# A macaron block of three stages in one kernel: flags summed behind the gate projection, products of the high halves first, and the order of prologue, first pass and tail

## The reference

```python
x = x + 0.5 * lora_experts(layernorm(x))     # stage 1
x = x + sparse_mlp(layernorm(x))             # stage 2
x = x + 0.5 * lora_experts(layernorm(x))     # stage 3

def lora_experts(x):        # 64 experts of rank 16, 16 of them chosen
    scores = x @ Wr.T
    gates = softmax of the 16 largest scores, 0 for the others
    h = einsum('nd,krd->nkr', x, A)
    return einsum('nkr,kdr->nd', h * gates, B) * 2.0

def sparse_mlp(x):          # 1376 hidden features
    s = silu(x @ w_gate.T)
    s = s with the 688 smallest |s| of each row set to 0
    return (s * (x @ w_up.T)) @ w_down.T
```

## Time and profile before

| | |
|---|---|
| median of 3 runs | 807.94 us (807.46 to 810.39) |
| the profiled execution | 808.51 us |
| its span, first to last instruction | 806.7 us |
| mean granted TensorE clock | 0.966 |
| busy: PE / DVE / ACT / POOL | 720.3 / 480.1 / 360.5 / 215.3 us |

### The profile page before, as it was taken

The page is one execution under the profiler, slowest core; times in us unless marked ns, Lnnn a source line. Parts: engine busy times, 40 slices in busy tenths (PEclk is TensorE's granted clock), DMA queues, the critical chain, the costliest instruction groups (busy, mean ns, idle before and its releaser), DMA issues.

```text
span 806.7 us, 10393 instructions
## 1 busy us (share of the span) xinstructions
PE 720.3 (89%) x3679; PEld 336.8 (42%) x3679; DVE 480.1 (60%) x1015; ACT 360.5 (45%) x447; POOL 215.3 (27%) x618
## 2 busy tenths in 40 slices
PE   4979877599999999999999999999999995899584
PEld 1434333244545444444444454444444442444231
DVE  5898492566566574756656666657565554554621
ACT  6936745252534435262525344352625252545200
POOL 4031404041323224050413232231504131323000
PEclk9999999699999999999999999999999998899897
DMA  9677203231534325352324343342522240403221
GB/s 336 150 195 204 45 9 61 31 84 28 100 53 90 66 63 91 63 87 55 79 47 85 49 89 65 69 73 63 79 59 45 52 76 1 101 14 76 62 53 39
DMA packets 170523, 62.28 MB, mean 77 GB/s; under 512 B 163632, under 2 KB 163632, under 8 KB 170464
## 3 DMA queue, kind: packets, MB, share of 16 engines
q1 hardware_dynamic: 167952, 51.01, 32.6%
q0 software_dynamic: 2512, 10.55, 3.5%
HBM read 16.97 MB, written 4.19 MB: 26 GB/s over the span
## 4 chain that ended last, share of the span: by engine, by line
DVE 32%; POOL 19%; issue 17%; PE 14%; ACT 12%; DMA 3%; DVEq 1%; SPq 0%; POOLq 0%; ACTq 0%
ACT signs L708 9%; POOL small L411 5%; PE ps L480 5%; PE ps L481 5%; PE ps L482 4%; POOL small L409 4%; DVE mem L999 3%; POOL small L408 3%; DVE small L1001 3%; DVE mem L979 3%; DVE mem L1018 3%; DVE stats L900 2%; DVE mem L1079 2%; POOL small L407 2%; ACT mem L726 2%
## 5 line engine op out<-in xcount | busy, mean ns | idle before, releaser
L708 ACT ACTIVATE signs<-mem,small 128x1376 bf16<-128x1376 f32 x112 | 161.5, 1442 | 146.7 <-POOL small L411 127.8
L480 PE MATMUL ps<-w_b_hi,pt_hi 128*128 128x512 f16 x256 | 99.0, 387 | 10.4 <-issue 9.8
L389 POOL TENSOR_SCALAR rvar<-mv 128x1 f32<-128x1 f32 x48 | 12.0, 249 | 338.6 <-DVE mv L901 337.6
L480 PE MATMUL ps<-w_a_hi,xt_f 128*128 128x512 f16 x256 | 99.5, 389 | 2.2 <-DVE w_a_lo L884 1.2
L481 PE MATMUL ps<-w_a_hi,xt_f 128*128 128x512 f16 x256 | 99.4, 388 | 0.0
L482 PE MATMUL ps<-w_a_lo,xt_f 128*128 128x512 f16 x256 | 99.0, 387 | 0.0
L481 PE MATMUL ps<-w_b_hi,pt_lo 128*128 128x512 f16 x256 | 98.8, 386 | 0.0
L482 PE MATMUL ps<-w_b_lo,pt_hi 128*128 128x512 f16 x256 | 98.8, 386 | 0.0
L480 PE MATMUL ps<-w_u_hi,xt 128*128 128x512 f16 (+1 forms) x192 | 69.3, 361 | 6.6 <-DVE mem L979 6.6
L480 PE MATMUL ps<-w_g_hi,xt 128*128 128x512 f16 (+1 forms) x192 | 70.2, 366 | 2.5 <-DVE mem L985 2.5
L692 ACT ACTIVATE mem<-mem 128x512 f16<-128x512 f32 x16 | 10.1, 629 | 137.2 <-DVE mem L907 137.2
(11 more groups left out here) (139 smaller groups left out, 1237.2 us busy)
## 6 DMA issues: line engine op xcount, KB each, us to landing
x<-x SPq DMA_DIRECT2D x14, 256.0 KB, 3.2
out<-x SPq DMA_DIRECT2D x14, 256.0 KB, 2.4
mem<-w_g POOLq DMA_DIRECT2D x4, 688.0 KB, 8.0
mem<-w_u POOLq DMA_DIRECT2D x4, 688.0 KB, 6.5
mem<-w_d POOLq DMA_DIRECT2D x5, 512.0 KB, 7.5
mem<-w_a SPq DMA_DIRECT2D x4, 512.0 KB, 6.0
mem<-w_b POOLq DMA_DIRECT2D x4, 512.0 KB, 6.4
pt_hi<-p_hi SPq DMA_TRANSPOSE x32, 3.2
```

The costliest lines, as they stand in the source:

```text
L480: pe.matmul(dst, x_hi, w_hi, start=start, stop=False)
L708: act.activation(signs[:, :], mags[t % 2], ACT.Sign, bias=thr, scale=-1.0, accum_out=bal).then_inc(counted, 1)
```

## The change

- `tile(d)` on TensorE: `gates(d + 2)` goes ahead of `sum_flags(d + 1)`. The other engines' lists are reordered with it: on ACT `tanh` goes ahead of `v_to_hi`, `magnitude` ahead of `exps`; on POOL `aim` ahead of `rstd(2, ...)`, with a new wait on `flag_ready`; on DVE `silu` stands right behind `check`, `norm_stats(2, ...)` behind `apply_route`.
- `combine` and `down` use `two_turned`: for all chunks first the two products that need only the high half of the turned operand, then the wait for the low half and the third products. The number of matmuls is the same.
- The squares of d move to `mem[:, 2 * IPAD:4 * IPAD]`, so `gated(0)` can stand ahead of `make_scale(MD)`; `mags[1]` changes places with the x slots and stage 3's buffers in `mem`.
- The prologue's order changes on all engines, and the first call `tile(0)` is written out with an order of its own.
- In the loop for d = 11 and 12, `rstd`, `x_to_hi` of stage 3 for the next tile are placed ahead of the last count, and DVE's `add_down`, `norm_apply`, `x_to_lo` and `add_ffn` ahead of `select`. In the tail one `x_to_lo` moves ahead of a `select`.
- The loads of u and d, already issued in a row by POOL, are not touched by any line of the diff.

```diff
@@ -130,16 +130,17 @@
         gate = mem[:, 4 * IPAD:4 * IPAD + I]
-        mags = [mem[:, 5 * IPAD:5 * IPAD + I], mem[:, AT_G + 4 * D:AT_G + 4 * D + I]]
-        assert 4 * IPAD >= DC * I and 5 * IPAD + I <= AT_G and 4 * D + I <= IC * D
+        mags = [mem[:, 5 * IPAD:5 * IPAD + I], mem[:, AT_G:AT_G + I]]
+        assert 4 * IPAD >= DC * I and 5 * IPAD + I <= AT_G and I + 4 * D <= IC * D
+        at_x = AT_G + I
...
         slots = [sb(f"x{n}", [P, D], F32)[:, :] for n in range(x_here)]
-        slots += [mem[:, AT_G + D * n:AT_G + D * (n + 1)] for n in range(2)]
+        slots += [mem[:, at_x + D * n:at_x + D * (n + 1)] for n in range(2)]
         normed = {j: sb(f"normed{j}", [P, D], F32)[:, :] for j in (1, 2)}
-        normed[3] = mem[:, AT_G + 2 * D:AT_G + 3 * D]
+        normed[3] = mem[:, at_x + 2 * D:at_x + 3 * D]
         halves = {j: sb(f"halves{j}", [P, 2 * D], F16)[:, :] for j in (1, 2)}
-        halves[3] = mem[:, AT_G + 3 * D:AT_G + 4 * D].bitcast(F16)
+        halves[3] = mem[:, at_x + 3 * D:at_x + 4 * D].bitcast(F16)
         xt_f = [sb(f"xt_f{n}", [P, 2 * DC, P], F16) for n in range(2)]
...
@@ -233,7 +234,7 @@
             place = {"r": signs[:, :], "a": hi["u"], "b": lo["u"], "g": hi["d"], "u": lo["d"],
-                     "d": mem[:, 0:2 * IPAD]}[m.name]
+                     "d": mem[:, 2 * IPAD:4 * IPAD]}[m.name]
             if m.name in "abgu":
...
@@ -312,8 +313,7 @@
                 turn_x(3, d)
-                if d >= 1:
-                    store(d - 1)
+                store(d - 1)
                 turn_v(d + 1)
...
@@ -344,9 +344,17 @@
             turn_x(1, 5)
+            turn_v(0)
             load_x(7)
-            turn_v(0)
-            for d in range(FULL):
+            turn_x(3, 0)
+            turn_p(number[1, LEAD])
+            turn_x(2, 3)
+            turn_x(1, LEAD + 1)
+            turn_v(1)
+            load_x(SLOTS - 1)
+            turn_p(number[3, 0])
+            for d in range(1, FULL):
                 tile(d)
...
@@ -396,6 +404,8 @@
                 pool.wait_ge(mag_ready, t + 1)
+                if t:
+                    pool.wait_ge(flag_ready, t)
                 pool.tensor_scalar(thr, mag_sum, GUESS, None, ALU.mult).then_inc(thr_ready, 1)
...
@@ -417,8 +427,8 @@
                 rstd(3, d)
+                aim(d + 2)
                 rstd(2, d + 3)
-                aim(d + 2)
                 search(d + 2, 0)
...
@@ -456,17 +466,25 @@
             aim(1)
-            searches(1, 0, 1, 2, 3, 4, 5)
-            for d in range(FULL):
+            searches(1, 0, 1, 2, 3)
+            rstd(3, 0)
+            searches(1, 4, 5)
+            aim(2)
+            rstd(2, 3)
+            search(2, 0)
+            rstd(1, LEAD + 1)
+            searches(2, 1, 2, 3, 4, 5)
+            for d in range(1, FULL):
                 tile(d)
+            rstd(3, FULL)
             for d in range(FULL, NT - 3):
-                rstd(3, d)
+                aim(d + 2)
                 rstd(2, d + 3)
-                aim(d + 2)
-                searches(d + 2, 0, 1, 2, 3, 4, 5)
-            rstd(3, NT - 3)
+                searches(d + 2, 0, 1, 2, 3, 4)
+                rstd(3, d + 1)
+                search(d + 2, 5)
...
@@ -543,18 +561,26 @@
+            def two_turned(dst, m, chunks, x_hi, x_lo, x_lo_loaded, upto, fresh=False):
+                for c in range(chunks):
+                    if fresh:
+                        split_done(m, c)
+                    pe.matmul(dst, x_hi[:, c, :], hi[m.name][:, c, :], start=c == 0, stop=False)
+                    pe.matmul(dst, x_hi[:, c, :], lo[m.name][:, c, :], start=False, stop=False)
+                pe.wait_ge(x_lo_loaded, upto)
+                for c in range(chunks):
+                    mm = pe.matmul(dst, x_lo[:, c, :], hi[m.name][:, c, :], start=False,
+                                   stop=c == chunks - 1)
+                return mm
...
                 pe.wait_ge(pt_hi_loaded, 16 * (k + 1))
-                pe.wait_ge(pt_lo_loaded, 16 * (k + 1))
                 if k:
                     pe.wait_ge(added, k)
-                for c in range(RC):
-                    if fresh:
-                        split_done(MB, c)
-                    mm = three(bank(COMB), MB, c, slice(0, D), pt_hi[k % 2][:, c, :],
-                               pt_lo[k % 2][:, c, :], c == 0, c == RC - 1)
-                mm.then_inc(combined, 1)
+                two_turned(bank(COMB), MB, RC, pt_hi[k % 2], pt_lo[k % 2], pt_lo_loaded,
+                           16 * (k + 1), fresh).then_inc(combined, 1)
...
@@ -584,11 +610,8 @@
                 pe.wait_ge(vt_hi_loaded, 16 * (t + 1))
-                pe.wait_ge(vt_lo_loaded, 16 * (t + 1))
-                for c in range(IC):
-                    mm = three(bank(DOWN), MD, c, slice(0, D), vt_hi[:, c, :], vt_lo[:, c, :],
-                               c == 0, c == IC - 1)
-                mm.then_inc(down_done, 1)
+                two_turned(bank(DOWN), MD, IC, vt_hi, vt_lo, vt_lo_loaded, 16 * (t + 1)
+                           ).then_inc(down_done, 1)
...
@@ -601,10 +624,9 @@
                 down(d)
-                if d:
-                    combine(3, d - 1)
+                combine(3, d - 1)
+                gates(d + 2)
                 sum_flags(d + 1)
-                gates(d + 2)
                 experts(1, d + LEAD)
...
@@ -627,15 +649,23 @@
             ups(0, fresh=True)
+            combine(1, 3)
             pe.wait_ge(scale_made, 5)
             norms(MD)
-            combine(1, 3)
             gates(1)
...
             ups(1)
-            for d in range(FULL):
+            down(0)
+            gates(2)
+            experts(1, LEAD)
+            ups(2)
+            sum_flags(1)
+            experts(3, 0)
+            combine(1, LEAD)
+            for d in range(1, FULL):
                 tile(d)
...
@@ -732,10 +762,10 @@
                 x_to_hi(3, d)
+                tanh(d + 2)
                 v_to_hi(d + 1)
-                tanh(d + 2)
+                magnitude(d + 2)
                 exps(number[1, d + LEAD])
-                magnitude(d + 2)
                 count(d + 2, 0)
...
@@ -781,9 +811,11 @@
             x_to_hi(2, 0)
+            square(MU, 0)
+            square(MU, 1)
             exps(3)
-            for n in range(len(MU.pieces)):
-                square(MU, n)
+            square(MU, 2)
+            square(MU, 3)
             p_to_hi(3)
...
@@ -808,31 +840,52 @@
             count(0, 6)
-            for n in range(1, len(MD.pieces)):
-                split_hi(MD, n)
-            x_to_hi(1, 5)
+            split_hi(MD, 1)
+            split_hi(MD, 2)
             tanh(1)
+            split_hi(MD, 3)
             magnitude(1)
+            split_hi(MD, 4)
+            split_hi(MD, 5)
             count(1, 0)
             v_to_hi(0)
-            counts(1, 1, 2, 3, 4, 5, 6)
-            for d in range(FULL):
+            x_to_hi(1, 5)
+            counts(1, 1, 2, 3, 4)
+            x_to_hi(3, 0)
+            count(1, 5)
+            tanh(2)
+            exps(number[1, LEAD])
+            count(1, 6)
+            magnitude(2)
+            p_to_hi(number[1, LEAD])
+            count(2, 0)
+            x_to_hi(2, 3)
+            x_to_hi(1, LEAD + 1)
+            count(2, 1)
+            v_to_hi(1)
+            exps(number[3, 0])
+            counts(2, 2, 3, 4)
+            p_to_hi(number[3, 0])
+            counts(2, 5, 6)
+            for d in range(1, FULL):
                 tile(d)
+            x_to_hi(3, FULL)
             for d in range(FULL, NT - 3):
-                x_to_hi(3, d)
+                tanh(d + 2)
                 v_to_hi(d + 1)
-                tanh(d + 2)
+                magnitude(d + 2)
                 exps(number[3, d])
-                magnitude(d + 2)
                 count(d + 2, 0)
...
                 x_to_hi(2, d + 3)
-                counts(d + 2, 2, 3, 4, 5, 6)
+                counts(d + 2, 2, 3, 4, 5)
+                x_to_hi(3, d + 1)
+                count(d + 2, 6)
             tanh(NT - 1)
-            x_to_hi(3, NT - 3)
             magnitude(NT - 1)
...
@@ -1081,27 +1134,25 @@
                 k1, k3 = number[1, d + LEAD], number[3, d]
-                if d:
-                    add_ffn(1, d + LEAD - 1)
+                add_ffn(1, d + LEAD - 1)
                 select(d + 1)
...
                 norm_stats(3, d)
+                add_ffn(3, d - 1)
                 norm_apply(3, d)
                 x_to_lo(3, d)
-                if d:
-                    add_ffn(3, d - 1)
                 check(d + 1)
+                silu(d + 2)
+                choose(k1)
                 v_to_lo(d + 1)
-                choose(k1)
-                silu(d + 2)
                 route(k1)
+                apply_route(k1)
                 norm_stats(2, d + 3)
-                apply_route(k1)
-                norm_apply(2, d + 3)
                 if d + LEAD + 1 < NT:
...
                 p_to_lo(k1)
+                norm_apply(2, d + 3)
```

(55 more changed lines are left out.)

## The result

The changed kernel takes 879.7 us (median of 4, 879.5 to 879.9) against 808.97 us before, a ratio of 1.0875 (95% interval 1.085 to 1.0899). 763 was forecast.

The account below looks back on a forecast made before the run. The loop through ACT, POOL and DVE, not TensorE's work, was taken to bound the middle. -12.2 - 14.0 - 14.8 - 0.7 - 3.9 = -45.6 against 808.51 gave 763.0 us, range 756 to 777.

Parts of the forecast that it names:

- part 2: COMB and DOWN, high halves first: covers waits for low halves, -3.9 us in the tail and -1.8 before UP(0).
- rival (d): Middle: chain from `check` to `select` outlasts the old 44.2 us period, FLAG stalls more; 815 us at 46.5; chance 0.03.
- 0.94 for faster: Whole kernel: chance that it gets faster by more than 0.5%, 4 us.
- Part 1: Middle: GATE ahead of FLAG cuts the loop through ACT, POOL and DVE; ten tiles of 42.6 us, -14.0 us.
- ten pauses: Middle: TensorE's waits before FLAG for `add_down`, some 1.5 us each, claimed to go with no new wait replacing them.
- The tightest margin, UP on `silu`: Middle tile: UP needs `silu` 24.9 us after DOWN's start and has it at 22.5, 2.4 us to spare.
- Part 3: Prologue and first pass, scheduled by hand: GATE(3) ends at 191.3 instead of 203.5, -12.2 us, -1.8 of it from part 2.
- Part 4: Tiles 11 and 12: the loop runs across two tiles, DOWN(13) starts 63.8 us after DOWN(11) instead of 78.6, -14.8 us.
- Part 5: Tail: UP(15) waits as before, FLAG(15) stays 5.8 us late, small shifts only, -0.7 us.
- the tail of part 2: Last tile: DOWN(15) gains 1.6 us, COMB(3,15) 1.25, and DOWN(15) perhaps 1 more of clock, -3.9 us.

Follow-up runs that it names:

- e11: The kernel before with the products of the high halves first and a select that repairs a threshold equal to a magnitude; engine lists as before: 803.19 us, ratio 0.9942.
- e9: The changed kernel with the repaired select and, in `tile` on TensorE, FLAG ahead of GATE again; other engines' lists as changed: 792.40 us, ratio 0.9801.
- e1: The changed kernel with the three products of each chunk added in the old order again in COMB and DOWN: 776.58 us, ratio 0.9623.
- the repaired kernel: The whole changed kernel with a select that can use a threshold equal to one magnitude, so no fallback for it: 768.82 us, ratio 0.9513.
- e10: The changed kernel with the repaired select and, in the loop for tiles 11 and 12, POOL's first search ahead of `rstd(2)`: 766.04 us, ratio 0.9475.
- e7: The run of the repaired kernel, the whole change plus a select that handles a threshold equal to one magnitude: 768.82 us, ratio 0.9513.

## Why the prediction was wrong, and where it was right

**The step that failed** is in part 2: "Where no wait stands, nothing changes: as many matmuls, at the same 0.215 us." That holds for TensorE, and e11 bears it out: DOWN takes 7.28 us in the middle with either order, and GATE(3) to GATE(13) is 439.5 us against 439.8. But the same products added in another order give other last bits, and this kernel has a branch that hangs on last bits: `select` compares float32 values for equality, `check` branches on the result. The prediction gave the branch no term: the trace of before never takes it. It costed `check` at 1.5 us of "read, branch and release" in all of its sums. Its other side stood in the code, 31 rounds each with one pass over 1,376 columns (1.65 us, as `select` and `mask` take in the earlier trace rows) and six small instructions: above 51 us from rows of before. Measured, the 31 rounds take 95.0 us (3.07 each) and the whole wait 112.2. No rival had it; the slower rival (d), a loop over 44.2 us, did not happen. The chance of 0.94 for faster rested on a proof of timing alone.

**Part 1, the middle: right.** -14.0 forecast, -14.7 measured (439.8 to 425.1). The prediction speaks of ten pauses; between GATE(3)'s end and GATE(13)'s the trace of before has nine, of 1.19 to 1.58 us, and the sum is right because it was taken from the ends of the stretch. That the waits would not come back in another place was the main claim, and they don't. The tightest margin, UP on `silu`, held: in the tile whose DOWN starts at 384.43, `silu` ends 22.6 us later (22.5 forecast) and UP starts after 24.8 (24.9). e9 shows that the gain needs GATE ahead of FLAG, and that the new lists of the other engines alone do not shorten the middle (447.7 us in the traced execution). GATE ahead with the old lists of the other engines was not run.

**Part 3, the first pass: right in its steps.** GATE(1) 95.6 (95.7 forecast), UP(1) 112.2 (113.4), DOWN(0) 126.8 (127.8), GATE(2) 135.8 (136.8), DOWN(1) 170.2 (170.5), GATE(3)'s end 191.2 (191.3). That the last of these agrees to 0.1 us is luck: 191.2 is the earliest of all, and in the other kernels with this prologue the end lies between 192.0 and 195.2. Their UP(0) starts at 81.1 in some and at 83 to 87 in others, so the 1.8 us that part 2 claims before UP(0) are shown by no run: e1, with the old order, has it at 83.3. That the transposes land at different times beside the bulk loads would explain the spread, but no run shows it. The clock fell after both waits as costed, e.g. nine slow matmuls after the 5.16 before DOWN(0).

**Part 4, tiles 11 and 12: mis-sized by 1.8.** In the repaired kernel DOWN(11) to DOWN(13) is 65.6 us, 63.8 forecast, 78.6 before. I had the counts of tile 13 end at 45.9; they end at 48.3, because POOL's `rstd(2)` ahead of the search and the slow `aim` delay count 1. Moving `rstd(2)` alone (e10) gives 64.2. The prediction names that queueing for the middle, where it is covered, and not here, where it isn't.

**Part 5 and the tail of part 2: mis-sized by 2.8, as the rest of two larger errors.** From DOWN(13)'s start to the last instruction it was 104.1 before, 99.5 forecast, and is 102.3 in the repaired kernel. DOWN(15) starts 1.02 late instead of 2.40 and COMB(3,15) 5.72 instead of 7.06, close to the forecast (1.6 and 1.25). But shorter waits give back more clock than the 1 us I had: part 2 is worth 5.7 us in the tail of the old order of work (104.1 to 98.4 in e11) and 6.0 in the new one (108.3 in e1 to 102.3), where I had 3.9. Part 5 went the other way: with the old sums the new order of work makes the tail 4.2 us longer (104.1 to 108.3), not 0.7 shorter. What was missed is FLAG(14), which didn't wait before and now waits 2.88 with half clock behind it, so that DOWN(14) starts 37.9 us after DOWN(13) instead of 33.8. I had set its counts 14.8 after DOWN(13)'s start, and they end 17.6 after it.

With the bisection out of the way the sum comes near: 768.3 and 768.8 measured, 763.0 forecast. In the trace of e7, 0.9 of the 4.8 us in the spans (765.9 against 761.1) is the first pass, 1.8 tiles 11 and 12, 2.8 the tail, and the middle gave 0.7 back.

## What to carry to other kernels

Before an accumulation is reordered, look for every place where values computed from it are compared for equality or steer a branch, and price the side that the trace never shows; a fallback that costs 14% of the kernel belongs in the forecast with its own price and chance. A rare case that a repair of one addition can settle should not be left to a fallback on the path of all engines. And when a margin is worked out for one regime of a schedule, work it out again for the shorter one: the POOL queue that was covered in the middle wasn't in tiles 11 and 12.

## What the runs showed of the hardware that I had not expected

- A POOL instruction on one column that starts beside a DVE instruction with two operands in SBUF lasts until that one ends. `aim`'s first instruction took 0.23 us (230 to 238 ns in all 16) in the kernel before and 1.60 us in 12 of 16 in the changed one; in each of the 12 it starts 0.1 us after `v_to_lo` and ends 0.1 us after it. The kernel before already shows the pattern: all 25 one-column instructions of POOL that start beside `p_to_lo` (1.22 us, both operands in SBUF) last until it has ended, as in the lines below, 1.19 us where the same instruction takes 0.19 by itself; of the 28 that start beside `apply_route` (1.22 us, one operand in PSUM) none is lengthened. This is read from the traces, no run isolates it. The Trainium skill (GPSIMD Engine Reference, 1. Specifications) says that GpSimd shares its SBUF interfaces with VectorE and contends with DVE instructions that have two SBUF inputs; `v_to_lo` has two, and the trace agrees.

```profile
257.29 1.23 DVE L959 TENSOR_TENSOR p_lo<-routed,p_hi 128x1024 f16<-128x1024 f32 x1 [1.41 <-ACT p_hi L703]
257.37 1.19 POOL L409 TENSOR_TENSOR small<-small 128x1 f32<-128x1 f32 x1
```

- None of the nine pauses of TensorE in the middle of the kernel before (1.19 to 1.58 us) was followed by slow matmuls. In the traced execution of e9 eight pauses were of 1.87 us and two of them were, by eight matmuls each (granted clock 0.51 from 234.0 to 237.5); the ninth, of 2.22 us, was not.
- Reordering floating-point additions moved the time of a kernel by 111 us (116 in the old order of work, 919.3 against 803.2), in every run: the inputs are fixed, so the hit is too, and no spread between runs gives it away.
